# A recurrence step in which one gating product moves from VectorE to GpSimd, by way of a copy on ScalarE

## The chip, the cores and the metric

The kernel runs on one core of one Trainium2 chip. The metric is the device time of one execution in microseconds (us), the median of several. The core has five engines that run side by side: TensorE (PE in the profile; its weight loads are PEld), VectorE (DVE), ScalarE (ACT), GpSimd (POOL) and SyncE (SP, here only for DMAs). They are kept in order by semaphores, which the kernel sets by hand.

## What is computed

Two layers, each a token mixer times a SiLU-gated mixture of experts, added to the input. Only layer 0 matters here. Its mixer is a recurrence over 32 chunks of 16 tokens, for 8 batches of 16 heads, and each chunk needs the state that the one before leaves:

```
k_h = softmax(k_t @ W_in) * lr ;  q_h = softmax(q_t @ W_in)
o_t = q_h @ W_out + (q_h k_h^T * mask) @ v_t
W_out = W_out + k_h^T v_t
for _ in range(2):
    g_out = -attn(W_in, k_t, v_t) ; g_in = -attn(W_out, v_t, k_t)
    W_in, W_out = W_in - lr_in * g_in, W_out - lr_out * g_out
```

Its experts have nothing to do with the recurrence. For each of 8 experts and the tokens sent to it:

```
gate = silu(x @ wg.T) ; up = x @ wu.T
y    = (gate * up) @ wd.T
```

The product `gate * up` is what the change is about.

## The kernel before

The recurrence is one long chain on VectorE: 32 steps `step(c, ...)`, one for each chunk, with small helps from the others. ScalarE takes the exponentials (`exp`, line 1319), TensorE sums over the head dimension (`q_sums`, `o_sums`, lines 955 and 963), GpSimd makes two products of 128x512 a step (`o_product`, line 529, after `qh_ready`, and `q_product`, line 524, after `p3_ready`).

The experts of layer 0 are laid into the gaps of steps 4 to 27 (FIRST = 4, AFTER = 28). The routed rows make 72 tiles of 128 rows, and each of these 24 steps takes TPS = 3 of them, k = 0, 1, 2. For one tile:

- TensorE transposes the rows (`xg_T`, line 921), ScalarE copies them (`xT`, line 1293).
- TensorE makes gate and up in two PSUM banks (`up`, lines 928 and 929), 1 + 2k and 2 + 2k; ScalarE takes the SiLU of the gate (`silu_gate`, line 1297) into `th[:, k]`.
- VectorE multiplies (`gated(k)`, line 1791): `hid[:, k] = th[:, k] * up`, reading `up` straight from PSUM, and signals `hid_ready`.
- TensorE transposes `hid` in four pieces (`hid_T`, line 935), ScalarE copies the result over `th[:, k]` (`hT`, line 1301), TensorE multiplies by `wd` (`down`, line 945), ScalarE scales the rows (`y`, line 1307), and GpSimd scatters them to DRAM (`y_scatter`, line 759).

Every engine works through its own list in the order written. Three lists matter.

VectorE, from the middle of a step to the middle of the next: the subtraction before the second exponential (1869), `q_softmax` (1832, 1834, which lets ScalarE take the exponential of `EQ`), `gated(0)`, then `Z2` and `G2` (1875, 1876), the division of `EQ` (1838, 1841, 1845, which lets GpSimd start `o_product`), a reduction (1879), `gated(1)`, three small operations on `WI` (1885 to 1890), the keys' product with `WI` and its reduction (1894, 1896), two maxima and two subtractions (1898 to 1902), `gated(2)`, and then, as the next step's beginning, `Z3` (1799), which waits for the exponentials of `E3`.

ScalarE: exponentials of `E3` and `EK`, `o_copy`, `y(c-1, 1)`, `xT(c, 2)`, `hT(c-1, 2)`, the packing of the values (1335) and of the keys (1336, into `KK`, which line 1894 reads), a table load, three `silu_gate` with `y(c-1, 2)` among them, a table load, the exponential of `E2`, `xT(c+1, 0)`, the exponential of `EQ`, `hT(c, 0)`, the paired values (1357), `y(c, 0)`, `xT(c+1, 1)`, `hT(c, 1)`. Then the next step's exponentials of `E3`.

TensorE, after `q_sums` of a step: `xg_T(c+1, 0)`, `hid_T(c, 0)`, `down(c, 0)`, `up(c+1, 0)`, `o_sums(c)`, `xg_T(c+1, 1)`, `hid_T(c, 1)`, `down(c, 1)`, `up(c+1, 1)`.

In the profile's names `th`, `hid` and `hidT` are all `xn` (they lie in one tile), `xgT` and `yg` are `xnT`, and `EQ`, `E2`, `E3`, the products and the sums are `x`; `KK` is `wproj`, and `G2`, `G3` are `cv`.

Of the kernel before, what the change touches and what calls it, by code (L numbers as in the profile page):

```python
# [9 lines left out]
ALU = mybir.AluOpType  # L10
ACT = mybir.ActivationFunctionType
# [19 lines left out]
TPS = 3  # L31
ROUTED_STEPS = TILES_A // TPS
FIRST = 4
AFTER = FIRST + ROUTED_STEPS
# [73 lines left out]
def build(nc, d):  # L108
# [5 lines left out]
    with ExitStack() as ctx:  # L114
# [3 lines left out]
        def sem(name):  # L118
            return ctx.enter_context(nc.semaphore(name))
# [15 lines left out]
        ps = ctx.enter_context(nc.psum_tensor("ps", [P, 8, 512], F32))  # L135
# [29 lines left out]
        K = sb("K", [P, HD, L])  # L165
# [43 lines left out]
        th, hid = r.take(TPS, F), r.take(TPS, F)  # L209
# [43 lines left out]
        KK, VC = r.take(2 * CH, HD), r.take(CH, HD)  # L253
# [105 lines left out]
        k_packed = sem("k_packed")  # L359
# [9 lines left out]
        xgT_copied = sem("xgT_copied")  # L369
        gu_ps = sem("gu_ps")  # L370
        gate_silu = sem("gate_silu")
        hid_ready = sem("hid_ready")
        hidT_ps = sem("hidT_ps")
        hidT_copied = sem("hidT_copied")
# [319 lines left out]
        def _(pool):  # L694
# [51 lines left out]
            def o_product(c):  # L746


                pool.wait_ge(qh_ready, c + 1)
                pool.wait_ge(o_ps, c + 1)  # L750
                op_of(pool).then_inc(op_ready, 1)

            q_product(FIRST)
            def y_scatter(c):

                for k in range(TPS):
# [3 lines left out]
                                            in_=yg[:, k, :], in_offset=None, bounds_check=2 * T - 1,  # L760
                                            oob_is_err=False).then_inc(y_stored[k], 16)

            for c in range(FIRST, NCH - 1):
                o_product(c)
                q_product(c + 1)
                if c < AFTER:
                    y_scatter(c)
# [81 lines left out]
        def _(pe):  # L849
# [80 lines left out]

            def hid_T(c, k):

                pe.wait_ge(hid_ready, c * TPS - FIRST * TPS + (k + 1))
                for f in range(FC):
                    t = pe.transpose(ps[:, 1 + 2 * k, f * P:(f + 1) * P], hid[:, k, f * P:(f + 1) * P], ident[:])  # L935
                t.then_inc(hidT_ps, 1)
# [264 lines left out]
        def _(act):  # L1201
# [97 lines left out]
            def hT(c, k):  # L1299
                act.wait_ge(hidT_ps, c * TPS - (FIRST * TPS - k - 1))  # L1300
                act.activation(hidT[:, k, :], ps[:, 1 + 2 * k, :], ACT.Copy).then_inc(hidT_copied, 1)  # L1301
# [11 lines left out]
            def packed(a, c, n):  # L1313
                return a[:, :, bass.ds(c * CH, n * CH)].rearrange("p e t -> p t e")

            def step(c, here, before=False, after=False, start=False, last=False, early=None, late=None):
                def exp(t, ready, done, scale=1.0):
                    act.wait_ge(ready, c + 1)
                    act.activation(t, t, ACT.Exp, scale=scale).then_inc(done, 1)  # L1319

                if start:
                    exp(E3[:, DI:2 * DI, :], rec_3, exp_3, temper)
                else:
                    exp(E3, rec_3, exp_3, temper)
                exp(EK, rec_k, exp_k)
                if not start:
                    o_copy(c - 1)
                if before:
                    y(c - 1, 1)
                if here:  # L1330
                    xT(c, 2)
                if before:
                    hT(c - 1, 2)
                if not last:
                    act.activation(VC, packed(V, c, 1), ACT.Copy).then_inc(v_packed, 1)
                    act.activation(KK, packed(K, c, 2), ACT.Copy).then_inc(k_packed, 1)
                if here:
                    act.preload_act_table(ACT.Silu)
                    silu_gate(c, 0)
                if before:  # L1340
                    y(c - 1, 2)
                if here:
                    silu_gate(c, 1)
                    silu_gate(c, 2)
                    act.preload_act_table(ACT.Exp)
                if early:
                    early()
                if not last:
                    exp(E2, rec_2, exp_2, temper)
                if after:  # L1350
                    xT(c + 1, 0)
                exp(EQ, rec_q, exp_q)
                if here:
                    hT(c, 0)
                if not last:

                    act.activation(VV.rearrange("p j (e l) -> p e j l", e=HD),
                                   V[:, :, bass.ds(c * CH, 2 * CH)].rearrange("p e (j l) -> p e j l", j=2), ACT.Copy).then_inc(v_pair, 1)
                if here:
                    y(c, 0)  # L1360
                if after:
                    xT(c + 1, 1)
                if here:
                    hT(c, 1)
                if late:
                    late()
# [243 lines left out]
        def _(dve):  # L1610
# [168 lines left out]
            def step(c, routed, first=False, last=False, alone=False, early=None, late=None):  # L1779
# [5 lines left out]
                def gated(k):  # L1785

                    if not routed:
                        return
                    dve.wait_ge(gate_silu, n0 + (k + 1))
                    dve.wait_ge(gu_ps, n0 * 2 + (2 * k + 2))  # L1790
                    tt(hid[:, k, :], th[:, k, :], ps[:, 2 + 2 * k, :], ALU.mult).then_inc(hid_ready, 1)  # L1791
# [76 lines left out]
                o.wait(m_2)  # L1868
                tt(E2, S2, bc(M2[:], 2, CH), ALU.subtract).then_inc(rec_2, 1)
                q_softmax()  # L1870
                gated(0)
                if late:
                    late()
                dve.wait_ge(exp_2, c + 1)
# [274 lines left out]
```

## Time and profile before

| | us |
|---|---|
| median of 3 runs | 1386.91 (1386.6 to 1388.56) |
| the profiled execution | 1388.35 |
| its span, first to last instruction | 1386.6 |
| VectorE busy in the span | 1236.4 (89%) |
| TensorE busy | 986.0 (71%) |
| ScalarE busy | 697.6 (50%) |
| GpSimd busy | 686.1 (49%) |
| mean granted TensorE clock | 0.860 of full speed |

The span runs from the first to the last instruction; 1.75 us of the profiled execution lie around it. Busy shares are averages over stages: the steps that carry expert tiles lie between about 228 and 700 us. A row of the timeline gives start, duration, engine, line, operation, output and inputs, and in brackets how long the engine had been idle and who released it. Consecutive operations of one engine overlap by about 0.1 us in these rows, so a slot is read from start to start.

### The profile page before, as it was taken

The numbers are of one execution on the slowest core, as the hardware profiler recorded it, in microseconds if no ns is written. First come the engines' busy times: TensorE is split into PE (matmuls) and PEld (weight loads), VectorE is DVE, ScalarE is ACT, GpSimd is POOL, SyncE is SP. The second block draws the span as 40 slices with busy tenths as digits, with TensorE's granted clock in tenths as the row PEclk, the third lists the DMA queues.
The fourth block names the chain that finished last, engine by engine and source line by source line (L and its number), as shares of the span: only waits on it lengthen the run. The fifth ranks groups of instructions, "written<-read, shape, count | busy, mean of one in ns | idle before, by whom it ended". The sixth has DMA issues, their size and how long they took to land. (4 is left out here: it accounts for less than half of the span.)

```text
span 1386.6 us, 15822 instructions
## 1 busy us (share of the span) xinstructions
PE 986.0 (71%) x3622; PEld 576.3 (42%) x3623; DVE 1236.4 (89%) x2319; ACT 697.6 (50%) x1319; POOL 686.1 (49%) x623
## 2 busy tenths in 40 slices
PE   3775233877777877777743587648898898888874
PEld 2142232555555555555533552224444343444331
DVE  6779895999999999999999978999897788979899
ACT  4563112455555455554432327537666667666751
POOL 5004772232223222222301006789798789788895
PEclk9877556899899899999975678979999999999998
DMA  9579211000000000000052305447434435444346
GB/s 305 153 205 312 69 46 32 20 22 19 19 22 21 19 17 19 22 23 18 6 154 91 91 1 178 130 120 200 178 139 151 152 127 173 154 157 163 109 171 186
DMA packets 106867, 145.49 MB, mean 105 GB/s; under 512 B 26443, under 2 KB 82520, under 8 KB 101952
## 3 DMA queue, kind: packets, MB, share of 16 engines
q1 hardware_dynamic: 91232, 118.70, 27.6%
q0 software_dynamic: 9920, 21.12, 4.3%
q10 hardware_dynamic: 5664, 5.11, 1.2%
q8 instruction: 16, 0.26, 0.1%
q14 instruction: 35, 0.29, 0.1%
HBM read 108.06 MB, written 39.04 MB: 106 GB/s over the span
## 5 line engine op out<-in xcount | busy, mean ns | idle before, releaser
L2041 DVE TENSOR_TENSOR ps<-ps,cv 128x512 f32<-128x512 f32 x256 | 163.2, 683 | 21.5 <-ACT ps L1570 20.6
L1106 PE MATMUL ps<-Q,ident 128*128 128x512 f32 x256 | 137.8, 630 | 35.5 <-DVE Q L2059 22.4
L759 POOL DMA_INDIRECT y_tok<-xnT,meta x72 | 75.4, 1048 | 175.2 <-ACT xnT L1307 160.7
L815 POOL TENSOR_TENSOR Q<-LR,xn 128x512 f32<-128x512 f32 x96 | 122.6, 1277 | 28.8 <-PE ps L1106 14.4
L736 POOL DMA_INDIRECT slots_x<-xn,sl_put x64 | 76.8, 1200 | 113.7 <-issue 113.4
L945 PE MATMUL ps<-wd_a,xn 128*128 x576 | 96.8, 319 | 36.7 <-ACT xn L1301 36.7
L945 PEld LDWEIGHTS ps<-wd_a,xn 128*128 128x128 f32 x576 | 81.9, 219 | 49.5 <-issue 48.0
L529 POOL TENSOR_TENSOR x<-x 128x512 f32<-128x512 f32 x27 | 31.8, 1176 | 141.7 <-DVE x L1845 141.7
L928 PE MATMUL ps<-wg_a,xnT 128*128 x144 | 91.1, 720 | 12.7 <-issue 11.6
L1319 ACT ACTIVATE x<-x 128x128 f32<-128x128 f32 (+1 forms) x127 | 31.9, 277 | 132.1 <-DVE x L1902 59.0
L963 PE MATMUL ps<-x,ident 128*128 128x128 f32 x256 | 43.1, 323 | 69.9 <-DVE x L529 36.8
L955 PE MATMUL ps<-x,ident 128*128 128x64 f32 x512 | 74.0, 298 | 26.4 <-DVE x L524 17.2
L2050 DVE TENSOR_TENSOR_SCAN LR<-V,ps 128x512 f32<-128x512 f32 x64 | 77.6, 1213 | 15.6 <-ACT V L1529 14.3
L955 PEld LDWEIGHTS ps<-x,ident 128*128 128x128 f32 x512 | 73.4, 218 | 40.9 <-DVE x L524 21.9
L1293 ACT ACTIVATE xnT<-ps 128x128 f32<-128x128 f32 x72 | 19.6, 272 | 130.5 <-PE ps L921 130.5
L935 PE MATMUL ps<-ident,xn 128*128 128x128 f32 x288 | 45.0, 279 | 56.5 <-DVE xn L1791 56.5
L1111 PE MATMUL ps<-Q,ident 128*128 128x512 f32 x144 | 79.2, 637 | 7.1 <-POOL Q L826 4.2
L2050 DVE TENSOR_TENSOR_SCAN LR<-wd_a,ps 128x512 f32<-128x512 f32 x64 | 77.6, 1212 | 5.6 <-ACT wd_a L1529 3.0
L1106 PEld LDWEIGHTS ps<-Q,ident 128*128 128x128 f32 x256 | 47.1, 198 | 81.2 <-DVE Q L2059 30.8
L929 PE MATMUL ps<-wu_a,xnT 128*128 x144 | 79.5, 636 | 0.0
L2050 DVE TENSOR_TENSOR_SCAN Q<-wd_a,ps 128x512 f32<-128x512 f32 x64 | 76.7, 1198 | 1.3 <-POOL seg L826 0.9
L963 PEld LDWEIGHTS ps<-x,ident 128*128 128x128 f32 x256 | 41.8, 236 | 86.5 <-DVE x L529 38.1
(343 smaller groups left out, 2807.2 us busy)
## 6 DMA issues: line engine op xcount, KB each, us to landing
cv<-bc_scr SPq DMA_DIRECT2D x64, 512.0 KB, 4.0
xn<-bc_scr SPq DMA_DIRECT2D x24, 1024.0 KB, 4.9
O<-bc_scr SPq DMA_DIRECT2D x8, 1024.0 KB, 5.7
slots_x<-O POOLq DMA_DIRECT2D x28, 260.0 KB, 5.6
qkv_scr<-cv SPq DMA_DIRECT2D x24, 256.0 KB, 4.7
xnT<-slots_x SPq DMA_DIRECT2D x72, 64.0 KB, 1.8
x<-in_x SPq DMA_DIRECT2D x8, 512.0 KB, 5.8
y_tok<-O SPq DMA_DIRECT2D x1, 4096.0 KB, 22.4
```

The source lines that it names most:

```text
L736: pool.indirect_dma_start(out=slots_x, out_offset=bass.IndirectOffsetOnAxis(ap=sl_put[:, j, i:i + 1], axis=0), in_=xn_rows[:, i, :], in_of ...
L759: pool.indirect_dma_start(out=y_tok, out_offset=bass.IndirectOffsetOnAxis(ap=meta_bits[:, n, 0:1], axis=0), in_=yg[:, k, :], in_offset=Non ...
L815: pool.tensor_tensor(yc_g0[:, n % 4, :], st_g0[:, n % 2, :], cn, ALU.mult).then_inc(yc_ready, 1)
L928: pe.matmul(ps[:, 1 + 2 * k, :], xgT[:, k, :], wg_a[:, bass.ds(off, F)], start=True, stop=True).then_inc(gu_ps, 1)
L929: pe.matmul(ps[:, 2 + 2 * k, :], xgT[:, k, :], wu_a[:, bass.ds(off, F)], start=True, stop=True).then_inc(gu_ps, 1)
L945: m = pe.matmul(ps[:, 0, 0:D], hidT[:, k, f * P:(f + 1) * P], wd_a[:, bass.ds(off + f * D, D)], start=(f == 0), stop=(f == FC - 1))
L955: m = pe.matmul(ps[:, 7, 0:DI * CH], ident[:], PQ[:, e, :, :], start=(e == 0), stop=(e == HD - 1))
L963: m = pe.matmul(ps[:, 7, 0:HD * CH], ident[:], OP[:, r, :, :], start=(r == 0), stop=(r == DI - 1))
L1106: pe.matmul(ps[:, 4, :], ident[:], yc_g0[:, n % 4, :], start=(n == 0), stop=(n == NS - 1)).then_inc(y0_used, 1)
L1111: pe.matmul(ps[:, 5, :], ident[:], yo_g1[(units_before(c) + u) % 3], start=(u == 0), stop=(u == units(c) - 1)).then_inc(y1_used, 1)
L2041: tt(dBu(g), ps[:, 2 + g, :], b_rows[:, n % 4, :], ALU.mult).then_inc((inject0, b_used)[g], 1)
L2050: dve.tensor_tensor_scan(st(n, g), dA(k), dBu(g), 0.0, ALU.mult, ALU.add).then_inc(scanned, 1)
```

## The change

Tile 0 of each of the 24 steps takes another way. ScalarE copies `up` from PSUM to `hid[:, 0]` behind the exponential of `EQ` and signals `u_copied`. GpSimd waits for that ahead of `o_product(c)`, multiplies `hid[:, 0]` by `th[:, 0]` in place and signals `hid0_ready`, for which `hid_T(c, 0)` now waits. VectorE's `gated(0)` is gone. Tiles 1 and 2 stay on VectorE. In these steps ScalarE packs the keys behind the new copy, no longer ahead of the table load.

```diff
+            def first_hidden(c):
+
+                pool.wait_ge(u_copied, c - FIRST + 1)
+                pool.tensor_tensor(hid[:, 0, :], th[:, 0, :], hid[:, 0, :], ALU.mult).then_inc(hid0_ready, 1)
+
             for c in range(FIRST, NCH - 1):
+                if c < AFTER:
+                    first_hidden(c)
                 o_product(c)
                 q_product(c + 1)
...
             def hid_T(c, k):
 
-                pe.wait_ge(hid_ready, c * TPS - FIRST * TPS + (k + 1))
+                if k == 0:
+                    pe.wait_ge(hid0_ready, c - (FIRST - 1))
+                else:
+                    pe.wait_ge(hid_ready, c * 2 - FIRST * 2 + k)
...
                     act.activation(VC, packed(V, c, 1), ACT.Copy).then_inc(v_packed, 1)
-                    act.activation(KK, packed(K, c, 2), ACT.Copy).then_inc(k_packed, 1)
+                    if not here:
+                        act.activation(KK, packed(K, c, 2), ACT.Copy).then_inc(k_packed, 1)
...
                 exp(EQ, rec_q, exp_q)
                 if here:
+                    act.activation(hid[:, 0, :], ps[:, 2, :], ACT.Copy).then_inc(u_copied, 1)
+                    act.activation(KK, packed(K, c, 2), ACT.Copy).then_inc(k_packed, 1)
                     hT(c, 0)
...
                 q_softmax()
-                gated(0)
                 if late:
                     late()
```

ScalarE in the loop over the steps with tiles, from the second table load on. Before:

```order
L1345 ACT_TABLE_LOAD
L1319 ACTIVATE x<-x 128x128
L1292 ISA
L1293 ACTIVATE xnT<-ps 128x128
L1319 ACTIVATE x<-x 128x64
L1300 REGISTER_ALU
L1301 ACTIVATE xn<-ps 128x512
```

Now (line 1367 is the copy of `up`, 1368 the keys' packing, 1313 is `hT(c, 0)`):

```order
L1358 ACT_TABLE_LOAD
L1331 ACTIVATE x<-x 128x128
L1304 ISA
L1305 ACTIVATE xnT<-ps 128x128
L1331 ACTIVATE x<-x 128x64
L1367 ACTIVATE xn<-ps 128x512
L1368 REGISTER_ALU
L1368 ACTIVATE wproj<-K 128x256
L1312 REGISTER_ALU
L1313 ACTIVATE xn<-ps 128x512
```

Two operations stand between the exponential of `EQ` and `hT(c, 0)`; the packing came from ahead of the first table load.

GpSimd, one step to the next. Before:

```order
L759 DMA y_tok<-xnT,meta 8192x128 x3
L529 TENSOR_TENSOR x<-x 128x512
L524 TENSOR_TENSOR x<-Q,WI 128x512
L759 DMA y_tok<-xnT,meta 8192x128 x3
L529 TENSOR_TENSOR x<-x 128x512
```

Now (line 768 is the new product, 531 and 526 are `o_product` and `q_product`):

```order
L761 DMA y_tok<-xnT,meta 8192x128 x3
L768 TENSOR_TENSOR xn<-xn 128x512
L531 TENSOR_TENSOR x<-x 128x512
L526 TENSOR_TENSOR x<-Q,WI 128x512
L761 DMA y_tok<-xnT,meta 8192x128 x3
```

The product stands behind the last step's three scatters and ahead of `o_product`.

VectorE at the same place, where only the product is gone. Before:

```order
L1834 TENSOR_TENSOR x<-ps,MQ 128x64
L1789 ISA
L1790 ISA
L1791 TENSOR_TENSOR xn<-xn,ps 128x512
L1875 TENSOR_REDUCE Z2Q<-x 128x8
L1876 REGISTER_ALU
L1876 TENSOR_TENSOR cv<-K,x 128x1024
L1838 TENSOR_REDUCE Z2Q<-x 128x16
```

Now:

```order
L1849 TENSOR_TENSOR x<-ps,MQ 128x64
L1889 TENSOR_REDUCE Z2Q<-x 128x8
L1890 REGISTER_ALU
L1890 TENSOR_TENSOR cv<-K,x 128x1024
L1853 TENSOR_REDUCE Z2Q<-x 128x16
```

`Z2`, `G2` and the sum of `EQ` follow `q_softmax` at once.

## Rows read from the trace of the kernel before

**Rows 1.** Busy time by stretch, the steps with tiles (PE, PEld, DVE, ACT, POOL, clock, DMA)

```profile
228.00:700.00 472.00, 362.51 (x1828) 253.72 (x1826) 449.20 (x913) 237.83 (x535) 131.15 (x121) 0.92 0.08 20
```

**Rows 2.** Groups by line, 228 to 690 us (busy, mean ns, idle before)

```profile
L1336 ACT ACTIVATE wproj<-K 128x256 f32 (+1 forms) x24 | 15.5, 644 | 0.0
...
L1799 DVE TENSOR_REDUCE Z3K<-x 128x8 f32<-128x128 f32 x24 | 6.8, 282 | 5.9 <-ACT x L1319 5.9
```

**Rows 3.** Timeline of VectorE, a step at full TensorE clock

```profile
527.33 0.23 DVE L1834 TENSOR_TENSOR x<-ps,MQ 128x64 f32<-128x64 f32 x1
527.56 0.69 DVE L1791 TENSOR_TENSOR xn<-xn,ps 128x512 f32<-128x512 f32 x1
528.17 0.28 DVE L1875 TENSOR_REDUCE Z2Q<-x 128x8 f32<-128x128 f32 x1
528.36 1.22 DVE L1876 TENSOR_TENSOR cv<-K,x 128x1024 f32<-128x1024 f32 x1
...
530.12 0.22 DVE L1845 TENSOR_TENSOR x<-x,Z2Q 128x64 f32<-128x64 f32 x1
...
536.85 0.28 DVE L1799 TENSOR_REDUCE Z3K<-x 128x8 f32<-128x128 f32 x1
```

**Rows 4.** Timeline of VectorE, a step without tiles

```profile
169.11 0.22 DVE L1834 TENSOR_TENSOR x<-ps,MQ 128x64 f32<-128x64 f32 x1
169.32 0.29 DVE L1875 TENSOR_REDUCE Z2Q<-x 128x8 f32<-128x128 f32 x1
```

**Rows 5.** Timeline of ScalarE, the step of rows 3

```profile
527.59 0.26 ACT L1319 ACTIVATE x<-x 128x64 f32<-128x64 f32 x1
529.00 0.60 ACT L1301 ACTIVATE xn<-ps 128x512 f32<-128x512 f32 x1 [1.16 <-PE ps L935]
...
534.53 0.60 ACT L1301 ACTIVATE xn<-ps 128x512 f32<-128x512 f32 x1 [0.16 <-PE ps L935]
536.37 0.45 ACT L1319 ACTIVATE x<-x 128x128 f32<-128x128 f32 x2 [1.24 <-DVE x L1902]
```

**Rows 6.** Timeline of TensorE, the step of rows 3

```profile
528.30 0.65 PE L935 MATMUL ps<-ident,xn 128*128 128x128 f32 x4 [2.00 <-DVE xn L1791]
529.72 1.15 PE L945 MATMUL ps<-wd_a,xn 128*128 x8 [0.77 <-ACT xn L1301]
```

**Rows 7.** Timeline of the next step, in which TensorE's clock falls: VectorE, ScalarE, TensorE

```profile
546.23 0.23 DVE L1834 TENSOR_TENSOR x<-ps,MQ 128x64 f32<-128x64 f32 x1
...
556.80 0.28 DVE L1799 TENSOR_REDUCE Z3K<-x 128x8 f32<-128x128 f32 x1 [0.96 <-ACT x L1319]
...
566.19 0.23 DVE L1834 TENSOR_TENSOR x<-ps,MQ 128x64 f32<-128x64 f32 x1
...
555.97 0.60 ACT L1301 ACTIVATE xn<-ps 128x512 f32<-128x512 f32 x1 [0.16 <-PE ps L935]
...
547.21 0.66 PE L935 MATMUL ps<-ident,xn 128*128 128x128 f32 x4 [3.00 <-DVE xn L1791]
...
548.63 2.07 PE L945 MATMUL ps<-wd_a,xn 128*128 x8 [0.76 <-ACT xn L1301]
```

**Rows 8.** Busy time by stretch, inside the step of rows 7 (columns as rows 1)

```profile
548.00:554.00 6.00, 5.37 (x13) 3.31 (x14) 5.70 (x11) 1.18 (x3) 2.06 (x2) 0.50 0.00 0
```

**Rows 9.** Timeline, a step with a short fall of the clock: VectorE, ScalarE

```profile
412.87 0.23 DVE L1834 TENSOR_TENSOR x<-ps,MQ 128x64 f32<-128x64 f32 x1
...
421.04 0.60 ACT L1301 ACTIVATE xn<-ps 128x512 f32<-128x512 f32 x1 [0.16 <-PE ps L935]
```

**Rows 10.** Timeline of GpSimd, the step of rows 3

```profile
530.43 1.18 POOL L529 TENSOR_TENSOR x<-x 128x512 f32<-128x512 f32 x1 [3.78 <-DVE x L1845]
```

**Rows 11.** Timeline, layer 1: products of VectorE and of GpSimd at one time

```profile
903.67 5.57 DVE L2059 TENSOR_TENSOR Q<-LR,O 128x512 f32<-128x512 f32 x1
...
903.76 2.49 POOL L771 TENSOR_TENSOR gateT<-gateT,V 128x512 f32<-128x512 f32 x2
906.19 2.49 POOL L775 TENSOR_TENSOR gateT<-gateT 128x512 f32<-128x512 f32 x2
```

More of the change, by code:

```diff
@@ L371, in build @@
         gate_silu = sem("gate_silu")
+        u_copied = sem("u_copied")
+        hid0_ready = sem("hid0_ready")
         hid_ready = sem("hid_ready")
```

## The prediction

> **What bounds the kernel now.** I read the busy times by stretch first. In the 472 us of the steps with tiles VectorE is busy 449 us, GpSimd 131 us and ScalarE 238 us [rows 1]. So VectorE looks like the whole bound, and an operation taken from it like pure gain. The groups by line show where VectorE still waits in those steps: at line 1799, for an exponential of ScalarE, 5.9 us in all [rows 2].
>
> That wait is the second thing to understand, so I followed one step on each engine's timeline. I count from the end of line 1834, at 527.56 [rows 3], and call it 0. VectorE begins the next step (line 1799) at 536.85, which is **+9.29**. ScalarE's last tile work ahead of the exponentials that line 1799 needs is `hT(c, 1)`, from 534.53, **+6.97**, and it then has 1.24 us with nothing to do [rows 5]. How `hT(c, 1)` comes about is TensorE's list: `hid_T(c, 0)` at 528.30 (+0.74), released by `gated(0)` [rows 6], then `down`, `up`, `o_sums`, `xg_T` and `hid_T(c, 1)`, which releases ScalarE's copy at +6.97 [rows 5]. Tile 1's product and `o_product` are done well before TensorE comes to them, so this is a chain of 6.2 us that begins with tile 0's product.
>
> The next step shows what happens when the chain is late. It begins after TensorE has been idle for 3.00 us, and TensorE then runs at granted clock 0.50, which is 1.2 GHz [rows 7, 8]. `down` takes 2.07 us, against 1.15 us in the step before [rows 6, 7]. `hT(c, 1)` starts at 555.97, +9.51 from 546.46, and line 1799 at 556.80, +10.34, after 0.96 us of idling [rows 7]. This gives a rule to count with: line 1799 starts **0.83 us** behind the start of `hT(c, 1)`, when that is what binds. ScalarE works in order and the exponentials stand behind `hT(c, 1)`.
>
> **Part 1: `gated(0)` leaves VectorE.** Its slot is 528.17 - 527.56 = 0.61 us [rows 3]. Line 1875 behind it needs an exponential from ScalarE. In the steps without tiles, where no product stands there, 1875 starts at 169.32 and 1834 ends at 169.33 [rows 4], so that exponential is in time. The slot is a full gain for VectorE: 24 x 0.61 = 14.6 us, if VectorE is all that counts. Line 1799 could then start at 9.29 - 0.61 = +8.68.
>
> **Part 2: ScalarE's copy.** The exponential of `EQ` starts at +0.03 [rows 5]. The copy is of the same kind and size as `hT`, 0.60 us, and since neighbours on ScalarE overlap (two exponentials, the second of 0.26 us, take 0.45 us together [rows 5]) it starts some 0.18 us after that one: +0.21 to +0.81. ScalarE is then waiting in any case until `hT(c, 0)` (1.16 us idle ahead of it [rows 5]), so its own time costs nothing. What matters is when it ends.
>
> **Part 3: the keys' packing.** It is 0.64 us [rows 2], moved into the same idle time, over by +1.5. VectorE's line 1894, which reads it, stands well behind line 1845 (+2.56 [rows 3]). Where it was it stood ahead of the table loads and the exponential of `E2`, which gain 0.64 us of room; VectorE does not wait there now (line 1875 [rows 3]), so it is worth nothing. Nor does it cost anything, since `hT(c, 0)` comes later than +1.5 now; if `hT(c, 0)` were ready at once, the packing would delay it by up to 0.6 us.
>
> **Part 4: GpSimd's product.** GpSimd follows a release by 0.09 us (line 1845 ends at 530.34, the product starts at 530.43 [rows 3, 10]), so it could start at +0.90. A product of 128x512 takes 1.18 us there [rows 10], and 1.25 us for two flat inputs (2.49 us for two [rows 11]); I take 1.27. What the trace of this layer does not show is such a product beside a VectorE operation that also reads two inputs from SBUF. Layer 1 does. VectorE's line 2059, 0.69 us of work, takes 5.57 us beside four products of GpSimd, and it ends 0.56 us behind their end (909.24 against 908.68) [rows 11]. So one waits for the other. In the changed step `G2` (line 1876, 1.22 us, two inputs in SBUF) runs from +0.19 to +1.41, right where the new product wants to start. If GpSimd waits for it, the product runs from +1.41 to +2.68. If not held up at all, it ends at +2.17. If it breaks in and VectorE waits, VectorE is 1.27 us late instead. I take the first, since VectorE was there first.
>
> The Trainium skill (GPSIMD Engine Reference, section 8, Key points) says the same in other words: GpSimd shares its SBUF interfaces with VectorE and contends with VectorE instructions that have two SBUF inputs. The trace agrees, by the 5.57 us of line 2059. By this rule the product's end is +2.68, without it +2.17.
>
> VectorE then meets the product itself: line 1845, which also has two inputs in SBUF, would start at 530.12 - 527.56 - 0.61 = +1.95 [rows 3] and waits until +2.68. That gives back 0.73 us, more than the 0.61 gained. Line 1799 by VectorE alone: 8.68 + 0.73 = +9.41. `o_product` behind it moves from +2.87 to some +3.0; TensorE reads it only after `up(c+1, 0)`, so this costs nothing.
>
> **Part 5: the chain.** `hid_T(c, 0)` starts 0.05 us behind the product: +2.73, where it was +0.74. The chain behind it shifts by **1.99 us** (by 1.48 without the port). `hT(c, 1)` starts at 6.97 + 1.99 = +8.96, and the exponentials that VectorE waits for stand behind it. Line 1799: 8.96 + 0.83 = **+9.8** (I take 9.83, with 7.0 for the undisturbed `hT`), against +9.29 now. So the step is 0.5 us longer even at full clock, and all of the gain is gone. What the shift does after 1799 I read in rows 7: there 1799 was already bound by `hT(c, 1)`, and the half step behind it took what it always takes, 9.6 us (556.80 to 566.42, the end of the next 1834 [rows 7]; 536.85 to 546.46 behind an unbound one [rows 3, 7]). No second stall is to be expected there.
>
> **Part 6: TensorE's clock.** In steps at full clock `hT(c, 1)` starts at about +7.0; in some the clock falls behind the idle time ahead of `hid_T(c, 0)`, and it starts 1.0 us later (421.04 - 413.10 = +7.94 [rows 9]) or 2.5 us later (+9.51 [rows 7]). Of the 23 steps that have a next tile, 8 were undisturbed, 9 about 1 us late and 6 about 2.5 us late. Now only the 6 cost anything, nearly all of the 5.9 us [rows 2], since the chain has slack. The slack is gone after the change, and each of these comes through in full. There are more of them too. All eight idle times of 3.0 us were followed by the low clock, the nine of 1.8 to 2.1 us by none ([rows 6, 7] show one of each kind). Six of 1.5 to 1.7 us, each behind a much delayed step, were followed by it too. In the changed step TensorE is done with its part of the next sums at about -0.75, as behind every delayed step now, and `hid_T` comes at +2.73: 3.5 us of idling in every step. So I expect the low clock in every step, at a mean of 1.0 and 2.5, that is 1.8 us.
>
> The Trainium skill (TensorE: Matmul & The Clock Gate, What's actually happening) holds that throttled is the default and activity releases it. By it longer idling can only lower the clock further; the falls behind the 3.00 us of rows 7 agree.
>
> **The sum.** The 23 steps now take from 1834's end to 1799 23 x 9.29 + 5.9 = 219.6 us. After: 23 x (9.83 + 1.8) = 267.5 us. The 24th step has no next `up` behind it and stays. Difference +47.9 us. On the profiled execution, 1388.35 us, that is **1436 us**. It lies 1.4 us above the median of the runs before, which is inside the uncertainty. Nothing outside the 24 steps changes; what follows moves with them.
>
> **The rivals.** (a) *The low clock stays as rare as it is*: the same 8, 9 and 6 steps, extra 9 x 1.0 + 6 x 2.5 = 24 us (with the port): 23 x 9.83 + 24 - 219.6 = +30, 1419 us. For it: some idle times were harmless. Against: none so long was. (b) *The port costs nothing*: shift 1.48, 1799 at +9.31 in a full-clock step, nearly where it was. With the clock as now 23 x 9.31 + 24 - 219.6 = +18.5, 1407 us; with the low clock in every step (idle time 3.0 us) 23 x (9.31 + 1.8) - 219.6 = +36, 1424 us. Against it stands only rows 11, from another place. (c) *Faster*: the chain is not what binds. 1799 takes the 0.61 us in all 24 steps, -14.6 us, 1374 us. It decides at `hT(c, 1)` starting by 8.68 - 0.83 = +7.85, so `hid_T(c, 0)` may come at most 0.9 us later than now. Copy and product one behind the other take 0.60 + 1.18 us [rows 5, 10], less the 0.69 that leaves; there is no row by which this fits. For it: the exponentials today wait for VectorE in 18 of 24 steps. (d) *It evens out within 0.2%*: no port and the clock rarely low. (e) *Longer low clock*: 2.5 us in every step, 23 x 12.33 - 219.6 = +64, 1452 us.
>
> **How the numbers follow.** About 0.2% (2.8 us) is what a measurement of this kernel can tell from no change. Forecast, low clock in every step and the port held: 0.43; (a) 0.16; (b) 0.22, both halves; (e) 0.09; (d) 0.04; (c) 0.06. Slower 0.90, same 0.04, faster 0.06. The predicted time is that of the forecast. The range takes in (a), (b) and most of (e), and leaves out (c) and (d): 1404 to 1450.
>
> **What would show it.** Right: what is line 1799 now waits for ScalarE in nearly all steps; `hT(c, 1)` some 9 us or more behind `q_softmax`; the new product ending 2.2 to 2.7 us behind it; `G2` or the division of `EQ` longer than 1.22 and 0.22 us; the granted clock in the stretch well below 0.92; steps of 19.4 us and more, where they are 18.9 now. Wrong: steps of 18.3 us, `hT(c, 1)` at or before +7.85, or full clock behind idle times of 3 us. If the steps are long though 1799 does not wait, the port is the cause and the chain is not.

## The result and the profile after

The changed kernel takes **1420.99 us** (median of 4 runs, 1418.53 to 1421.39) against 1387.74 us for the kernel before on the same chip (4 runs, 1386.6 to 1388.98). The ratio is 1.0232, with a 95% interval from 1.0216 to 1.0249: it is slower by 33 us.

| | before | after |
|---|---|---|
| median, us | 1387.74 | 1420.99 |
| the profiled execution | 1388.35 | 1421.39 |
| its span | 1386.6 | 1419.6 |
| from one `q_softmax` to the next, steps 4 to 27 (23 intervals), together | 440.75 | 472.01 |
| the same, one interval | 18.90 in 17 of 23, 19.8 to 20.0 in the others | 20.45 in 19 of 23, 20.8 to 21.2 in the others |
| VectorE busy in the span | 1236.4 (89%) | 1233.5 (87%) |

The interval behind step 27 grows as well, from 18.88 to 20.41 us. With it the steps with tiles are 32.8 us longer, and that is all of the span's 33.0.

Busy time by stretch of the changed kernel, the steps with tiles (columns as in rows 1):

```profile
228.00:733.00 505.00, 371.42 (x1832) 261.35 (x1831) 446.58 (x890) 248.58 (x559) 166.53 (x145) 0.90 0.07 18
```

Against [rows 1] the stretch is 33 us longer, and VectorE is busy for 446.6 us of it instead of 449.2. The 24 products that left were worth 16.6 us of busy time, but the division of `EQ` now takes 10.5 us more, and that is waiting inside an instruction, which the profile counts as busy (see below). GpSimd has 35 us more. So the 33 us went into waiting. Which wait it is stands in the groups by line, VectorE, 228 to 725 us (busy, mean ns, idle before, and what ended it):

```profile
L1806 DVE TENSOR_TENSOR xn<-xn,ps 128x512 f32<-128x512 f32 x48 | 32.4, 676 | 0.0
...
L1860 DVE TENSOR_TENSOR x<-x,Z2Q 128x64 f32<-128x64 f32 x24 | 15.9, 662 | 0.8
...
L1814 DVE TENSOR_REDUCE Z3K<-x 128x8 f32<-128x128 f32 x25 | 7.1, 285 | 40.2 <-ACT x L1331 40.0
```

Line 1814 is what 1799 was. Its wait for the exponentials of `E3` was 5.9 us [rows 2] and is now 40.2 us, 34.3 more. Line 1860, the division of `EQ`, takes 0.66 us on average, and 0.22 us in [rows 3]. And GpSimd's groups in the same stretch:

```profile
L768 POOL TENSOR_TENSOR xn<-xn 128x512 f32<-128x512 f32 x24 | 39.9, 1664 | 54.2 <-ACT xn L1367 54.2
L531 POOL TENSOR_TENSOR x<-x 128x512 f32<-128x512 f32 x24 | 28.4, 1183 | 3.9 <-DVE x L1860 3.9
```

The new product (line 768) takes 1664 ns, while `o_product` (line 531), of the same shape, takes 1183 ns. Now one step in order of time. VectorE (start us, length us), counted as in the prediction from the end of `q_softmax`'s subtraction (line 1849), at 548.46:

```profile
548.24 0.22 DVE L1849 TENSOR_TENSOR x<-ps,MQ 128x64 f32<-128x64 f32 x1
548.44 0.29 DVE L1889 TENSOR_REDUCE Z2Q<-x 128x8 f32<-128x128 f32 x1
548.65 1.21 DVE L1890 TENSOR_TENSOR cv<-K,x 128x1024 f32<-128x1024 f32 x1
...
550.40 0.66 DVE L1860 TENSOR_TENSOR x<-x,Z2Q 128x64 f32<-128x64 f32 x1
...
559.30 0.28 DVE L1814 TENSOR_REDUCE Z3K<-x 128x8 f32<-128x128 f32 x1 [1.65 <-ACT x L1331]
```

ScalarE in the same step:

```profile
548.66 0.58 ACT L1367 ACTIVATE xn<-ps 128x512 f32<-128x512 f32 x1
549.13 0.64 ACT L1368 ACTIVATE wproj<-K 128x256 f32 x1
...
551.73 0.60 ACT L1313 ACTIVATE xn<-ps 128x512 f32<-128x512 f32 x1 [1.95 <-PE ps L947]
...
558.47 0.60 ACT L1313 ACTIVATE xn<-ps 128x512 f32<-128x512 f32 x1 [0.16 <-PE ps L947]
558.96 0.45 ACT L1331 ACTIVATE x<-x 128x128 f32<-128x128 f32 x2
```

GpSimd:

```profile
549.32 1.66 POOL L768 TENSOR_TENSOR xn<-xn 128x512 f32<-128x512 f32 x1 [1.84 <-ACT xn L1367]
551.14 1.18 POOL L531 TENSOR_TENSOR x<-x 128x512 f32<-128x512 f32 x1 [0.16 <-DVE x L1860]
```

TensorE:

```profile
551.04 0.66 PE L947 MATMUL ps<-ident,xn 128*128 128x128 f32 x4 [3.35 <-POOL xn L768]
552.46 1.94 PE L957 MATMUL ps<-wd_a,xn 128*128 x8 [0.76 <-ACT xn L1313]
554.19 1.91 PE L937 MATMUL ps<-wg_a,xnT 128*128 x2
555.90 1.10 PE L938 MATMUL ps<-wu_a,xnT 128*128 x2
```

Line 947 is `hid_T`, 957 is `down`, and the second 1313 row is `hT(c, 1)`. Read together: the copy of `up` runs at once (+0.20 to +0.78), the product from +0.86 to +2.52, `hid_T(c, 0)` follows at +2.58 after TensorE has been idle for 3.35 us, and `hT(c, 1)` comes at +10.01 (it was +6.97). VectorE is ready 1.65 us before line 1814 may start, at +10.84. That is 0.83 us behind `hT(c, 1)`, as in [rows 7]. The matmuls behind the idle time are slow: 1.94 us for `down` against 1.15 in [rows 6]. The granted clock in slices of 2 us shows it:

```profile
550.00:552.00 2.00, 0.66 (x4) 0.42 (x4) 1.93 (x4) 0.27 (x1) 1.84 (x2) 1.00 0.00 0
552.00:554.00 2.00, 1.54 (x8) 1.55 (x9) 1.80 (x6) 0.63 (x2) 0.33 (x1) 0.66 0.00 0
554.00:556.00 2.00, 2.00 (x5) 0.97 (x5) 1.97 (x2) 0.37 (x1) 1.08 (x1) 0.50 0.00 0
556.00:558.00 2.00, 2.00 (x14) 1.52 (x13) 1.58 (x6) 0.00 (x0) 1.02 (x2) 0.99 0.08 33
```

The clock is at 0.50, which is 1.2 GHz, for 3.4 us. Such a stretch lies at this place in 19 of the 24 steps. In the other five (4, 5, 13, 22 and 27) the clock is low for 6.8 us or more. The result is two things laid one on the other, the later start of the chain (1.83 us) and the lower clock in it (10.01 - 7.0 - 1.83 = 1.18 us). What follows tells them apart by experiment.

### The profile page after: what moved, and what is told of

The parts are those of the page before. It is cut to its first block and busy times, and to the rows that moved or that the text cites. A ratio compares the mean times of both kernels' runs of the same rounds, so it can differ in the third digit from the quotient of the medians.

```text
span 1419.6 us, 15864 instructions
## 1 busy us (share of the span) xinstructions
PE 992.8 (70%) x3622; PEld 582.5 (41%) x3623; DVE 1233.5 (87%) x2295; ACT 708.1 (50%) x1343; POOL 720.5 (51%) x647
## 5 line engine op out<-in xcount | busy, mean ns | idle before, releaser
L761 POOL DMA_INDIRECT y_tok<-xnT,meta x72 | 70.7, 982 | 217.3 <-ACT xnT L1319 206.7
L738 POOL DMA_INDIRECT slots_x<-xn,sl_put x64 | 76.5, 1196 | 114.8 <-issue 114.6
L957 PE MATMUL ps<-wd_a,xn 128*128 x576 | 103.6, 336 | 36.7 <-ACT xn L1313 36.7
L957 PEld LDWEIGHTS ps<-wd_a,xn 128*128 128x128 f32 x576 | 87.8, 233 | 50.1 <-issue 48.7
L937 PE MATMUL ps<-wg_a,xnT 128*128 x144 | 98.3, 772 | 10.4 <-issue 9.3
L967 PEld LDWEIGHTS ps<-x,ident 128*128 128x128 f32 x512 | 73.4, 218 | 40.4 <-DVE x L526 21.9
L1305 ACT ACTIVATE xnT<-ps 128x128 f32<-128x128 f32 x72 | 19.5, 271 | 129.3 <-PE ps L930 129.3
L2064 DVE TENSOR_TENSOR_SCAN Q<-V,ps 128x512 f32<-128x512 f32 x64 | 76.5, 1196 | 0.0
L802 POOL DMA_INDIRECT slots_x<-xn,sl_put x64 | 65.2, 1019 | 20.3 <-issue 18.4
L938 PE MATMUL ps<-wu_a,xnT 128*128 x144 | 75.4, 605 | 0.0
```

The source lines that it names most:

```text
L738: pool.indirect_dma_start(out=slots_x, out_offset=bass.IndirectOffsetOnAxis(ap=sl_put[:, j, i:i + 1], axis=0), in_=xn_rows[:, i, :], in_of ...
L761: pool.indirect_dma_start(out=y_tok, out_offset=bass.IndirectOffsetOnAxis(ap=meta_bits[:, n, 0:1], axis=0), in_=yg[:, k, :], in_offset=Non ...
L802: pool.indirect_dma_start(out=slots_x1, out_offset=bass.IndirectOffsetOnAxis(ap=sl_put[:, j, i:i + 1], axis=0), in_=xn_rows[:, i, :], in_o ...
L937: pe.matmul(ps[:, 1 + 2 * k, :], xgT[:, k, :], wg_a[:, bass.ds(off, F)], start=True, stop=True).then_inc(gu_ps, 1)
L938: pe.matmul(ps[:, 2 + 2 * k, :], xgT[:, k, :], wu_a[:, bass.ds(off, F)], start=True, stop=True).then_inc(gu_ps, 1)
L957: m = pe.matmul(ps[:, 0, 0:D], hidT[:, k, f * P:(f + 1) * P], wd_a[:, bass.ds(off + f * D, D)], start=(f == 0), stop=(f == FC - 1))
```

## The experiments

Each kernel ran on one chip, beside runs of the kernel before on that chip. Ratios are against those, with their 95% interval. A "step" is the time from one `q_softmax` to the next, and the last column is the sum of the same 23 steps as in the first table (440.75 before, 472.01 after).

| label | us | before, same chip | ratio | 23 steps, us |
|---|---|---|---|---|
| e1_packing_only | 1388.49 | 1388.57 | 1.000 (0.998 to 1.002) | 441.46 |
| e2_early_copy | 1380.45 | 1388.57 | 0.995 (0.993 to 0.997) | 430.84 |
| e3_exps_first | 1422.02 | 1388.57 | 1.024 (1.022 to 1.026) | 472.96 |
| e5_g2_behind | 1424.20 | 1388.57 | 1.026 (1.024 to 1.029) | 471.89 |
| e4_after_filled | 1394.75 | 1387.93 | 1.005 (1.003 to 1.007) | 445.58 |
| e6_before_filled | 1385.16 | 1387.93 | 0.998 (0.997 to 0.999) | 435.25 |
| e7_early_timed | 1374.66 | 1400.30 | 0.982 (0.980 to 0.984) | 425.83 |
| e8_early_timed_pack | 1384.08 | 1400.30 | 0.988 (0.985 to 0.992) | 424.02 |
| e9_g2_behind_filled | 1412.67 | 1400.30 | 1.010 (1.007 to 1.012) | 451.37 |
| e10_early_timed_again | 1375.16 | 1388.45 | 0.990 (0.988 to 0.992) | 424.78 |
| e11_early_timed_filled | 1366.26 | 1388.45 | 0.985 (0.983 to 0.987) | 420.36 |

On the chip of e7 to e9 the kernel before took 1400.3 us, some 12 us more than on all others. The last column, from each trace, is not touched by what happens outside the steps, so kernels that ran on different chips are compared by it.

### e1: the packing alone

The kernel before, with the keys' packing moved to where the change has it.

```diff
-                    act.activation(KK, packed(K, c, 2), ACT.Copy).then_inc(k_packed, 1)
+                    if not here:
+                        act.activation(KK, packed(K, c, 2), ACT.Copy).then_inc(k_packed, 1)
...
                 exp(EQ, rec_q, exp_q)
                 if here:
+                    act.activation(KK, packed(K, c, 2), ACT.Copy).then_inc(k_packed, 1)
                     hT(c, 0)
```

> The kernel before, with only the keys' packing moved behind the exponential of EQ (no copy, no product on GpSimd). Theory (packing is hidden in both places): hT(c, 0) still starts 1.4 us behind the end of q_softmax, steps stay 18.9 us, time within 0.2% of the kernel before, about 1387 us. Rival (the packing delays the tile chain or the keys' product): some 0.1 to 0.6 us a step, up to 1400 us.

Measured: 1388.49 against 1388.57 us. One step of ScalarE (line 1355 is the packing, 1301 is `hT(c, 0)`):

```profile
527.17 0.63 ACT L1355 ACTIVATE wproj<-K 128x256 f32 x1
528.42 0.60 ACT L1301 ACTIVATE xn<-ps 128x512 f32<-128x512 f32 x1 [0.62 <-PE ps L935]
```

The packing is over 0.62 us before `hT(c, 0)` starts, and `hT(c, 0)` starts at +1.44 as before. The packing fits into ScalarE's idle time, and part 3 of the prediction holds.

### e2: the copy and the product a third of a step earlier

ScalarE copies as soon as gate and up of tile 0 are there, behind the first `silu_gate`, and GpSimd multiplies ahead of the last scatter of the step before.

```diff
                     silu_gate(c, 0)
+                    act.wait_ge(gu_ps, c * (2 * TPS) - (FIRST * 2 * TPS - 2))
+                    act.activation(hid[:, 0, :], ps[:, 2, :], ACT.Copy).then_inc(u_copied, 1)
...
                 exp(EQ, rec_q, exp_q)
                 if here:
-                    act.activation(hid[:, 0, :], ps[:, 2, :], ACT.Copy).then_inc(u_copied, 1)
...
+            first_hidden(FIRST)
             for c in range(FIRST, NCH - 1):
-                if c < AFTER:
-                    first_hidden(c)
                 o_product(c)
                 q_product(c + 1)
                 if c < AFTER:
-                    y_scatter(c)
+                    y_scatter(c, range(2))
+                    if c + 1 < AFTER:
+                        first_hidden(c + 1)
+                    y_scatter(c, (2,))
```

> The changed kernel, with ScalarE's copy of the up projection and GpSimd's product moved ahead: the copy right behind the first silu_gate, the product ahead of the last scatter, so that it is done before q_softmax instead of 2.5 us behind it. Theory (the late product starts a chain TensorE - ScalarE that ends in the exponentials VectorE waits for, and what costs is where the product stands, not that it is on GpSimd): hid_T(c, 0) no longer waits, the wait ahead of the first reduction of a step nearly goes, VectorE keeps its 0.61 us a step: about 1387 - 14.6 - up to 5 = 1367 to 1374 us. Rival (a product on GpSimd costs VectorE its SBUF port or its neighbours on ScalarE time wherever it stands): no faster than before, 1387 to 1400 us.

Measured: 1380.45 us, less than before but not the 1367 to 1374 expected. The wait at the first reduction is gone (0.1 us in 23 steps), and nine of the 23 steps are 18.28 us, about 18.90 - 0.61. So the slot in VectorE's list is worth what part 1 says, once the chain is out of the way. But eight steps are 19.34 to 19.41 us, and the rest 18.4 to 18.7. The timeline of one of the eight, GpSimd and VectorE:

```profile
536.15 1.27 POOL L768 TENSOR_TENSOR xn<-xn 128x512 f32<-128x512 f32 x1 [3.35 <-ACT xn L1356]
```

```profile
536.22 1.24 DVE L1877 COPY WO<-x 128x32 f32<-128x32 f32 x1
```

A copy of 128x32 of VectorE takes 1.24 us beside GpSimd's product, and ends 0.04 us behind it. The answer by source line gives the shortest, the median and the longest of 31 in ns:

```profile
L1877 DVE COPY WO<-x x31: 186/186/1260, 145.6 to 731.7; 128x32 f32<-128x32 f32 x31
```

Eight of the 31 copies took 1.22 to 1.26 us, one in each of the eight long steps. The copy reads one operand only, from SBUF into SBUF. The hold is therefore wider than "two inputs in SBUF", which is how I had put it, and it takes 1.05 us from the gain wherever the product falls there.

### e3: the next exponentials ahead of hT(c, 1)

The changed kernel; only ScalarE's order changes, so that what line 1814 waits for no longer stands behind `hT(c, 1)`.

```diff
                 exp(EK, rec_k, exp_k)
+                if before:
+                    hT(c - 1, 1)
...
-                if here:
-                    hT(c, 1)
```

> The changed kernel, with ScalarE's hT(c, 1) moved behind the next step's exponentials of E3 and EK, so that these no longer stand behind it. Theory A (only ScalarE's order binds): VectorE starts the next step at about +9.1 us behind q_softmax instead of +10.8, steps of 18.7 us, about 1421 - 23 x 1.7 = 1382 us. Theory B (TensorE's chain is as long as the step, about 20.2 us of 20.45, and the wait only moves): the wait turns up at q_softmax or at the exponential of E2, steps of about 20.2 us, 1415 us or more.

Measured: 1422.02 us, as slow as the changed kernel. VectorE's groups, 228 to 735 us:

```profile
L1814 DVE TENSOR_REDUCE Z3K<-x 128x8 f32<-128x128 f32 x25 | 7.1, 286 | 24.1 <-ACT x L1331 24.1
...
L1889 DVE TENSOR_REDUCE Z2Q<-x 128x8 f32<-128x128 f32 x24 | 6.9, 286 | 6.2 <-ACT x L1331 6.2
...
L1847 DVE TENSOR_REDUCE MQ<-ps 128x16 f32<-128x64 f32 x25 | 5.6, 224 | 8.3 <-PE ps L967 8.3
```

The 40.2 us of waiting became 38.6, in three places: still the exponentials of `E3`, and now TensorE's sums (line 1847) and the second exponential (1889) too. Some of the wait did move, then, to what stands later in TensorE's and ScalarE's lists, and the time is the one that theory B gave. But 24.1 us stayed at line 1814, and ScalarE's timeline shows why (one step; line 1305 is `xT`, 1331 the exponentials):

```profile
559.11 0.28 ACT L1305 ACTIVATE xnT<-ps 128x128 f32<-128x128 f32 x1 [2.79 <-PE ps L930]
559.42 0.46 ACT L1331 ACTIVATE x<-x 128x128 f32<-128x128 f32 x2
```

The exponentials now stand behind `xT(c+1, 1)`, which waits for the transposes that TensorE makes just ahead of `hid_T(c, 1)`. In the changed kernel that copy starts only 0.44 us ahead of `hT(c, 1)`. So this edit took the exponentials 0.44 us forward in the chain and not out of it. What would happen with the exponentials ahead of both copies was not tried, so that no order of ScalarE's list can help is not shown.

### e4 and e6: TensorE kept busy ahead of hid_T(c, 0)

Matmuls whose result nobody reads stand where TensorE would be idle, 4 of them in the changed kernel (e4), 2 in the kernel before (e6).

```diff
                     if here:
+                        if k == 0:
+                            pe.wait_ge(gate_silu, c * TPS - (FIRST * TPS - 1))
+                            for _ in range(4):
+                                pe.matmul(ps[:, 1, :], ident[:], wg_a[:, 0:F], start=True, stop=True)
                         hid_T(c, k)
```

> The changed kernel, with four unneeded matmuls of 512 columns on TensorE ahead of hid_T(c, 0), into the PSUM bank that hid_T overwrites next: they fill most of the 3.3 us in which TensorE waits for GpSimd's product. Theory (over a third of the loss is TensorE's clock, which falls behind that idle time in every step): the low stretches go, hT(c, 1) comes at +8.8 instead of +10.0 us behind q_softmax, steps of 19.3 us instead of 20.45, 23 x 1.18 = 27 us less, about 1394 us. Rival (the low clock has another cause, or costs nothing): no change, 1421 us, or slower where the filling runs over.

> The kernel before, with two such matmuls (some 1.3 us) ahead of hid_T(c, 0), where TensorE idles 1.5 to 3.0 us. Theory: the low stretches of 3.4 and 6.8 us go in most steps, the waits at the first reduction of a step (5.9 us in all) with them: 1382 us. Rival: the clock falls as before, 1387 us, and nothing is gained.

Measured, e4: 1394.75 us, 26 less than the changed kernel, as expected. Busy time by stretch, VectorE's group at the first reduction, and one step (its end of `q_softmax` at 548.94, then `hT(c, 1)` at +8.81):

```profile
228.00:704.00 476.00, 417.54 (x2018) 267.28 (x2016) 445.86 (x885) 249.10 (x558) 165.77 (x144) 0.99 0.08 20
```

```profile
L1818 DVE TENSOR_REDUCE Z3K<-x 128x8 f32<-128x128 f32 x25 | 7.1, 285 | 13.5 <-ACT x L1335 13.5
```

```profile
548.72 0.22 DVE L1853 TENSOR_TENSOR x<-ps,MQ 128x64 f32<-128x64 f32 x1
...
557.75 0.60 ACT L1317 ACTIVATE xn<-ps 128x512 f32<-128x512 f32 x1 [0.16 <-PE ps L947]
```

The clock goes from 0.90 to 0.99, TensorE's busy time rises by 46 us, and the 23 steps become shorter by 26.4 us. Nothing else was touched, so those 26 us are the price of the low clock in the changed kernel: 23 x 1.18 = 27. The steps of some 19.27 us that remain (all but the first) are the late start of the chain alone: 7.0 + 1.83 is +8.83 for `hT(c, 1)`, and +8.81 was measured.

Measured, e6: 1385.16 us, 3 us less than before (5 were expected). All steps but the first (19.5) are 18.9 us, and the wait at the first reduction is 0.9 us instead of 5.9:

```profile
L1803 DVE TENSOR_REDUCE Z3K<-x 128x8 f32<-128x128 f32 x25 | 7.0, 279 | 0.9 <-ACT x L1323 0.9
```

The low clock did not go as the theory said. The 6.8 us stretches are gone but for the first step. In nine of the other 22 steps the clock is still low for 3.4 us, behind idle times of only 1.2 to 1.3 us. In these steps `hT(c, 1)` comes at +8.05 to +8.51, and the slack up to line 1803 hides all but 0.04 us of it in one of them. The 23 steps are 5.5 us shorter than before (435.25 against 440.75); why the whole kernel gains only 3 was not followed up.

e4 and e6 together split the loss. In the 23 steps the changed kernel loses 31.3 us (472.01 - 440.75). Of these, 26.4 are its low clock, and 4.8 are what the late chain at full clock costs against the kernel before (445.58 - 440.75), which itself loses 5.5 us to its low clock.

### e5 and e9: GpSimd's product freed from G2

In the changed kernel `G2` goes behind the division of `EQ`, so that it does not run while GpSimd's product starts. e9 is e5 with the four matmuls of e4.

```diff
-                g_2 = o.mark(tt(G2, bc(kc, 1, 2 * DI), bc(E2, 2, HD), ALU.mult))
                 q_apply(q_sum())
+                g_2 = o.mark(tt(G2, bc(kc, 1, 2 * DI), bc(E2, 2, HD), ALU.mult))
```

> The changed kernel, with VectorE's product G2 (1.22 us, two inputs in SBUF) moved behind the division of EQ, so that it does not run when GpSimd's product wants to start. Theory (GpSimd waits until G2 is through): the product takes 1.1 us instead of 1.66, ends at +2.0 instead of +2.5 us behind q_softmax, the chain starts 0.55 us earlier, the division waits for the product instead; 0 to 0.55 us a step less, about 1408 us if TensorE's low clock stays the same. Rival (1.66 us is what this product takes in any case): no change, 1421 us, or slower by what G2's new place costs.

> The changed kernel with both edits: G2 behind the division, and four unneeded matmuls ahead of hid_T(c, 0). With TensorE at full clock the port can be priced by itself, against the filled run alone (1394.8 us). Theory (GpSimd waits 0.40 us for G2 in every step and the whole chain with it): product from +0.86 to +2.12, hT(c, 1) 0.4 us earlier, 23 x 0.40 = 9 us less, 1385 to 1386 us. Rival (the port costs nothing on the chain, only the clock did): 1395 us.

Measured, e5: 1424.20 us, where 1408 was expected. GpSimd's and VectorE's groups in the steps with tiles:

```profile
L768 POOL TENSOR_TENSOR xn<-xn 128x512 f32<-128x512 f32 x24 | 30.3, 1261 | 54.5 <-ACT xn L1367 54.5
```

```profile
L1860 DVE TENSOR_TENSOR x<-x,Z2Q 128x64 f32<-128x64 f32 x24 | 30.0, 1248 | 0.8
...
L1814 DVE TENSOR_REDUCE Z3K<-x 128x8 f32<-128x128 f32 x25 | 7.1, 286 | 20.1 <-ACT x L1331 20.1
```

and the busy time by stretch:

```profile
228.00:735.00 507.00, 382.33 (x1835) 266.65 (x1835) 467.14 (x892) 248.92 (x559) 178.95 (x145) 0.86 0.07 18
```

The product is back to 1261 ns from 1664: the hold by `G2` is real and costs 0.40 us. `hid_T(c, 0)` came 0.41 us earlier, as it should. But two things took that back. The division now meets the product in full and takes 1.25 us instead of 0.66. And the clock is low for longer, 0.86 instead of 0.90, with `hT(c, 1)` at +9.7 to +10.3 in all but the first step, though the chain started earlier.

Measured, e9, without the low clock: `hT(c, 1)` at +8.41, 0.40 earlier than e4's +8.81, so the hold is worth 0.40 us of the chain. Still the step is 19.57 us, 0.30 longer than e4's, since VectorE is now the one that is late. It reaches line 1818 at +9.96, where in e4 it would have been ready at +9.19. Of these 0.77 us, 0.59 are the longer division:

```profile
L1864 DVE TENSOR_TENSOR x<-x,Z2Q 128x64 f32<-128x64 f32 x24 | 30.0, 1248 | 0.8
...
L1818 DVE TENSOR_REDUCE Z3K<-x 128x8 f32<-128x128 f32 x25 | 7.0, 279 | 1.5 <-ACT x L1335 1.5
```

GpSimd's `o_product` (line 531) in turn now meets the moved `G2` (line 1895), and takes 2.10 us instead of 1.18:

```profile
539.15 1.21 DVE L1895 TENSOR_TENSOR cv<-K,x 128x1024 f32<-128x1024 f32 x1
539.31 2.10 POOL L531 TENSOR_TENSOR x<-x 128x512 f32<-128x512 f32 x1 [0.17 <-DVE x L1864]
```

Expected were 1385 us; I had counted the chain and not the 1.25 us of the division. By the 23 steps e9 is 5.8 us slower than e4. Its 1412.67 us hold some 10 us more that lie behind the steps: from the `q_softmax` of step 31 to the end e8 and e9 take 638 to 639 us, e7 and e10 628 to 629. VectorE idles some 14 us at one line of layer 1 (2079) in e8 and e9, and 1 us in e7. The cause is not known.

### e7, e10 and e8: the early product at a time where nothing collides

e2 with one more wait, that lets GpSimd start when VectorE's product with `WO` is done. Beside it then run reductions. e8 also puts `hT(c, 0)` ahead of the packing.

```diff
                 pool.wait_ge(u_copied, c - FIRST + 1)
+                pool.wait_ge(dve_order, 332 + (c - FIRST) * 28 + 14)
```

> The early copy and product, with one more wait: GpSimd's product starts only when VectorE's product of the second attention (two inputs in SBUF) is through, so that it runs beside a reduction and a maximum with one input each. In the run without this wait ten steps were 1.05 us longer, where the product ran beside a copy of VectorE of 128x32 that took 1.24 us instead of 0.19. Theory (the port is all that is left): every step 18.3 us, VectorE's copy 0.19 us and the product 1.27 us in all of them, 1387 - 24 x 0.61 - 5.5 = 1367 us. Rival (the added wait makes hid_T(c, 0) late, or something else holds those steps): 1380 us as without it.

> The timed early product once more, since the runs of the kernel before beside the first measurement lay 12 us above all others. In the steps with tiles it gained 15 us, and nothing else is changed: 1387 - 15 = 1372 us, a ratio of 0.989. Rival (the ratio of 0.982 is the edit's): 1362 us.

> As the timed one, with the keys' packing behind hT(c, 0) instead of ahead of it. hT(c, 0) starts 0.5 us earlier, +0.2 instead of +0.7 us behind q_softmax. Theory (the chain has slack again): no change, 1367 us within 0.2%. Rival (the chain still binds in steps at TensorE's low clock): up to 0.3 us in those, 2 to 3 us less.

Measured: e7 1374.66 us, and e10, the same kernel on another chip, 1375.16 us; 1367 and 1372 were expected. The ratio of e7 (0.982) leans on the 1400.3 us of the kernel before beside it; e10's 0.990 is the one to trust. The VectorE copy and GpSimd's product in e7, by source line and by group:

```profile
L1878 DVE COPY WO<-x x31: 186/186/189, 147.1 to 726.1; 128x32 f32<-128x32 f32 x31
```

```profile
L769 POOL TENSOR_TENSOR xn<-xn 128x512 f32<-128x512 f32 x24 | 30.5, 1272 | 111.9 <-DVE x L1882 87.5 <-ACT xnT L1322 24.4
```

The copy is never held (189 ns at most, 1260 in e2; in e2 it was eight steps, not the ten that the expectation of e7 names), though the product's 1272 ns lie wholly beside VectorE's reductions. Steps are 18.27 to 18.7 us, not all 18.3: VectorE still waits 3.4 us in all for the second exponential and 0.8 us at the first reduction, in steps in which TensorE's clock is low. e8's are much the same (424.02 us for 23 against 425.83 and 424.78), so the packing's place is worth next to nothing here as well; its total of 1384.08 us (1367 were expected) comes from layer 1, as said above.

### e11: the same with the clock held up

e8 with two of e6's matmuls.

```diff
                     if here:
+                        if k == 0:
+                            pe.wait_ge(gate_silu, c * TPS - (FIRST * TPS - 1))
+                            for _ in range(2):
+                                pe.matmul(ps[:, 1, :], ident[:], wg_a[:, 0:F], start=True, stop=True)
                         hid_T(c, k)
```

> The timed early product with the packing behind hT(c, 0), and two unneeded matmuls of 512 columns ahead of hid_T(c, 0). Theory (what is left above 18.3 us a step, some 0.2 us in the mean and up to 0.4 us, is TensorE at the low clock, through xT(c + 1, 0), which stands ahead of the exponential of EQ on ScalarE): every step 18.3 us, 4 to 5 us less than without the filling, 1367 us. Rival (the low clock is hidden now, or the filling holds up hid_T): 1372 us or more.

Measured: 1366.26 us, 22 us less than the kernel before beside it and 55 less than the changed one. Busy time by stretch, and the group at the first reduction:

```profile
228.00:690.00 462.00, 382.63 (x1939) 252.55 (x1939) 444.04 (x906) 250.40 (x564) 161.72 (x147) 0.99 0.10 26
```

```profile
L1822 DVE TENSOR_REDUCE Z3K<-x 128x8 f32<-128x128 f32 x26 | 7.2, 278 | 0.8 <-ACT x L1338 0.8
```

Every step is 18.27 us, 9.61 for its second half and 8.66 for its first (the prediction's 8.68 for VectorE alone), with `hT(c, 1)` at +5.72. That is the 1367 us expected. The steps' 20.4 us against before (440.75 - 420.36) are 23 x 0.61 = 14 and the stall's 5.9, as counted. The idea of the change, one product off VectorE, is good for what part 1 says. The 33 us are the cost of the place that it was given.

## Why the prediction was off by 15 us

It said 1436 us, from 1404 to 1450, slower with a chance of 0.90. Measured: 1421. The direction, the wait (line 1814 for ScalarE, in every step) and the chain behind it were as forecast. Two terms of the sum were too large, above all the price of the low clock.

- **Part 1, the slot of 0.61 us**: right, and shown by e11's steps.
- **Parts 2 and 3, copy and packing free**: right (+0.20 to +0.78; e1).
- **Part 4, the product waits for `G2`**: right in kind. `G2` ends at +1.40, the product at +2.52, so behind `G2` it took 1.12 us, not 1.27. The 1.27 is what the product takes when nothing holds it (1.26 in e5, 1.27 in e7); held, it has 0.14 us less to do once `G2` is over. Division of `EQ`: end forecast +2.9, measured +2.60, because it ends only 0.08 us behind the product. VectorE alone would be ready at some +9.2 (10.84 - 1.65), forecast +9.41. The Trainium skill (GPSIMD Engine Reference, section 8, Key points) names the shared interfaces; the trace agrees, by 1664 against 1261 ns in e5.
- **Part 5, the chain's shift**: forecast 1.99 us, measured 1.83 (`hid_T(c, 0)` at +2.58 instead of +2.73). Over 23 steps, with line 1814 at 7.0 + 1.83 + 0.83 = +9.66 instead of +9.83: **3.9 us too much**.
- **Part 6, the low clock in every step**: right. What failed is its price, "a mean of 1.0 and 2.5, that is 1.8 us". It is 1.18 us in 19 of the 23 steps, the short kind of [rows 9] each time, and e4 puts it at 26 us in all. 23 x 0.62 = **14.3 us too much**. Even in the four steps with 6.8 us of low clock or more, `hT(c, 1)` comes only 0.3 to 0.8 us later than that, and not 1.5. The mean over the mixed falls of before was no estimate of the falls in the changed kernel, which are nearly all alike. Why they are alike is not shown: in e5 the idle times are alike too (2.9 to 3.0 us), and there the falls come in a pattern of three steps, two of 6.8 us and one of 3.4.
- **The sum**: 267.5 us forecast for the 23 first halves, 250.9 measured; 14.3 + 3.9 is 18.2, and 1.6 us go back, nearly all of it in the four steps with the longer low clock (4, 5, 13 and 22), which take 20.8 to 21.2 us. "The 24th step stays" was wrong by 1.5 us. Its first half did stay (line 1814 at +9.33), but in its second half VectorE waits 1.61 us for the packed values, which ScalarE makes behind `hT(c, 2)`, and that comes late behind 5.33 us of TensorE's next task. I had counted one wait of that step only.

Of the rivals, (a) with 1419 and (b) with 1424 are nearer in time than my forecast, and both are wrong in what they say: the clock was low in every step, and the port did hold. A number that fits is no support for its mechanism; e4 and e5 are. Rival (c), 1374, is what e10 reaches when the product starts early enough.

## What to carry to other kernels

When work moves from a busy engine to an idle one, ask first who waits for its result, and how long copy and product take one behind the other: 0.61 us of the bound engine were exchanged for 1.83 us on a chain that had 1.5 us to spare. Give the moved work a start that is early by a margin, and beside reductions of the other engine (e7), which were not held. And where TensorE idles at the same place of every step, price that idle time by a run with unneeded matmuls in it (e4, e6) before believing any sum over its chain.

## What was new about the hardware

- GpSimd's product of 128x512 and VectorE's products of two SBUF inputs wait for one another: the later one goes on when the earlier one is over, not at half speed beside it. The product behind `G2` ends 0.40 us later; `o_product` beside the moved `G2` takes 2.10 us instead of 1.18 (e9); a division of 128x64 takes 0.66 or 1.25 us instead of 0.22, according to how much of the product is left; and a plain copy of 128x32, with one input, took 1.24 instead of 0.19 (e2). In e7 reductions of VectorE ran beside the product at no cost to either (1.22 and 1.27 us).
- A low clock can come back in every step. With some 3.3 us of idle time a step TensorE ran at 0.50 for 3.4 us at the same place in 19 of 24 steps, and for longer in the others. Making the idle time 0.4 us shorter (e5, 3.0 us) did not shorten the low stretches, it made them 6.8 us in most steps. With idle times of 1.2 to 1.3 us (e6) the clock still fell for 3.4 us in nine steps of 23, and in others it did not. So the length of the idle time alone did not tell what followed. Filling the idle time with 3.6 us of unneeded matmuls (e4) removed the low stretches in all steps but the first (clock 0.99), and the kernel became 26 us faster with TensorE 46 us busier. Why e5's stretches are longer stays open.
